# Squares of q and k laid out by head in a fused two-block transformer kernel, and the sums over them on VectorE

## The reference, cut to what matters

```python
def _l2norm(t):                     # HEADS = 16, EPS = 1e-12
    n = jnp.sqrt(jnp.sum(t * t, axis=-1, keepdims=True))
    return t / jnp.maximum(n, EPS)
q, k, v = (proj(Wq), proj(Wk), proj(Wv))   # (b, head, token, 8)
q = _l2norm(q)
k = _l2norm(k)
sim = jnp.einsum('bhid,bhjd->bhij', q, k) * SCALE
```

## Time and profile before

| | |
|---|---|
| median of 3 runs | 1092.72 us (1090.68 to 1095.87) |
| the profiled execution | 1093.79 us, of which the span from first to last instruction is 1092.0 us |
| granted TensorE clock, mean | 0.951 of full speed |
| busy: PE, DVE, ACT, POOL | 946.0, 877.3, 768.5, 281.8 us |
| sums of squares, line 1175 | 32 instructions, 32.4 us |
| squares, line 972 | 32 instructions, 19.3 us |

### The profile page before, as it was taken

One profiled execution on the slowest core, in us unless ns is written; L12 is line 12 of the kernel. 1 busy time (PEld: TensorE's weight loads), 2 busy tenths in 40 slices (PEclk: granted clock), 3 DMA queues, 4 the chain that ended last, 5 costly groups with the idle time before them and its releaser, 6 DMA issues.

```text
span 1092.0 us, 37313 instructions
## 1 busy us (share of the span) xinstructions
PE 946.0 (87%) x15889; PEld 516.0 (47%) x15889; DVE 877.3 (80%) x2112; ACT 768.5 (70%) x1042; POOL 281.8 (26%) x264
## 2 busy tenths in 40 slices
PE   4687978888989899999999999998989899899694
PEld 1333444444544445454555545454545455455352
DVE  3977767889788898989899898989898888864633
ACT  2165557677767778787777778887777778788581
POOL 6111213223133131322223132223223232222212
PEclk8598889899999999999999999999999999999797
DMA  5243413455417062442617162543628170405220
GB/s 148 76 97 99 119 45 85 118 127 129 128 57 189 22 190 57 138 119 84 172 48 198 36 186 54 144 106 104 152 69 186 41 195 22 119 3 127 72 57 20
DMA packets 94342, 112.95 MB, mean 103 GB/s; under 512 B 15200, under 2 KB 81888, under 8 KB 94176
## 3 DMA queue, kind: packets, MB, share of 16 engines
q1 hardware_dynamic: 94176, 110.56, 38.6%
HBM read 55.22 MB, written 54.53 MB: 100 GB/s over the span
## 4 chain that ended last, share of the span: by engine, by line
PE 44%; DVE 31%; ACT 15%; issue 6%; POOL 1%; DMA 1%; SPq 0%; DVEq 0%; POOLq 0%; ACTq 0%
PE acc L729 14%; DVE rowmax L1081 11%; ACT prob L930 10%; PE pool L712 6%; PE pool L595 4%; PE pool L643 4%; PE pool L762 3%; DVE xn L1039 3%; PE pool L784 3%; PE pool L609 3%; DVE stats L1027 2%; PE pool L770 2%; PE pool L659 2%; DVE rest_k L1052 2%; PE pool L681 2%
## 5 line engine op out<-in xcount | busy, mean ns | idle before, releaser
L930 ACT ACTIVATE prob<-pool 128x1024 f32<-128x1024 f32 x576 | 565.3, 1030 | 136.3 <-PE pool L659 132.8
L1081 DVE TENSOR_REDUCE rowmax<-pool 128x2 f32<-128x1024 f32 (+7 forms) x480 | 357.2, 791 | 64.9 <-PE pool L659 62.2
L729 PE MATMUL acc<-prob,vals_a 128*32 128x512 f32 (+7 forms) x2048 | 167.7, 422 | 0.2 <-ACT prob L930 0.2
L729 PE MATMUL acc<-prob,vals_b 128*32 128x512 f32 (+7 forms) x2048 | 162.8, 418 | 1.5 <-DVE turned_b L1117 1.1
L643 PE MATMUL pool<-stack_ka,stack_qa 48*64 48x512 bf16 (+7 forms) x2048 | 117.0, 301 | 39.7 <-ACT prob L930 12.7
L712 PE MATMUL pool<-stack_qa,stack_ka 51*64 51x512 bf16 (+7 forms) x2048 | 113.3, 301 | 32.6 <-DVE rowmax L1081 18.4
L659 PE MATMUL pool<-mask_t,ident_b 64*64 64x128 bf16 (+1 forms) x2304 | 129.5, 215 | 0.0
L712 PE MATMUL pool<-stack_qb,stack_kb 48*64 48x512 bf16 (+7 forms) x2048 | 112.4, 295 | 17.1 <-ACT prob L930 8.3
L643 PEld LDWEIGHTS pool<-stack_ka,stack_qa 48*64 48x64 bf16 x2048 | 42.8, 108 | 131.8 <-issue 46.8
L1292 POOL TENSOR_TENSOR rstd<-mv,minus_half 128x4 f32<-128x4 f32 x64 | 65.4, 1022 | 146.1 <-DVE mv L1034 146.1
L712 PEld LDWEIGHTS pool<-stack_qa,stack_ka 51*64 51x64 bf16 x2048 | 42.8, 108 | 88.2 <-issue 26.3
(11 more groups left out here) (129 smaller groups left out, 1380.5 us busy)
## 6 DMA issues: line engine op xcount, KB each, us to landing
stack_qa<-scratch_qa SPq DMA_DIRECT2D x64, 192.0 KB, 4.9
stack_ka<-scratch_ka SPq DMA_DIRECT2D x64, 192.0 KB, 4.9
stack_kb<-scratch_kb SPq DMA_DIRECT2D x64, 192.0 KB, 3.9
stack_qb<-scratch_qb SPq DMA_DIRECT2D x64, 192.0 KB, 4.8
scratch_qa<-parts_q SPq DMA_DIRECT2D x16, 384.0 KB, 2.8
scratch_ka<-parts_k SPq DMA_DIRECT2D x16, 384.0 KB, 4.8
scratch_qb<-parts_q SPq DMA_DIRECT2D x16, 384.0 KB, 2.6
scratch_kb<-parts_k SPq DMA_DIRECT2D x16, 384.0 KB, 2.9
```

Of the source, the lines that this page charges most:

```text
L729: last = eng.matmul(acc[32 * j:32 * j + 32, BLK * blk:T], vals[a][:, blk, GROUP * g + j, :], prob[n % NPROB][:, k, at:at + T - BLK * blk], ...
L930: eng.activation(prob[n % NPROB][:, :, :], place["unit", n][0][:, :, :], ACT.Exp, scale=scale).then_inc(S["exped"], 1)
L1081: last = eng.tensor_reduce(to, of, axis=AX.X, op=ALU.max)
```

## The change

The squares are written in the order (h d), a head's 8 components side by side, while they are read from PSUM in the order (d h) as they stand there. The sum reads them in the order in which they now lie. Nothing else is changed: the copy `raw`, the result `qk` of line 1207, all instruction counts, waits and the order of the steps are the same.

```diff
@@ class Scalar, project_qk @@
                     q.wait_ge(S["qk_made"], 2 * b + half + 1)
-                    eng.activation(qk[:, two, :, :].rearrange("p k a c -> p k (a c)"),
-                                   ps[:, :].rearrange("p (k c) -> p k c", k=2), ACT.Square)
+                    eng.activation(qk[:, two, :, :].rearrange("p k a (h d) -> p (k a) d h", d=D),
+                                   ps[:, :].rearrange("p (ka d h) -> p ka d h", d=D, h=HEADS), ACT.Square)
                     eng.activation(raw[:, two, :, :].rearrange("p k a c -> p k (a c)"),
                                    ps[:, :].rearrange("p (k c) -> p k c", k=2), ACT.Copy).then_inc(S["raw_qk"], 1)
@@ class Vector, project_qk @@
                     last = eng.tensor_reduce(
                         ssum[:, w * half:w * (half + 1)].rearrange("p (k h) -> p k h", k=4),
-                        qk[:, two, :, :].rearrange("p k a (d h) -> p (k a) h d", d=D), axis=AX.X, op=ALU.add)
+                        qk[:, two, :, :].rearrange("p k a (h d) -> p (k a) h d", d=D), axis=AX.X, op=ALU.add)
```

## The result

The changed kernel takes 1102.31 us (median of 4 runs, 1101.71 to 1103.76), against 1093.37 us before (median of 4 runs, 1090.68 to 1095.87): a ratio of 1.0086, with a 95% interval of 1.0061 to 1.0112. It is slower by about 9 us, where I had forecast 2.4 us less. The range ended at 1096 us, so the result lies outside it, at the rival that I had given 0.08.

A forecast was written before the change was run, and what follows sets the result against it. No engine is full; the chain runs 44% on PE, 31% on DVE, 15% on ACT. Seven shorter sums at four places save 2.45 us, 1093.79 to 1091.3 us (1090.3 for the median); range 1085.5 to 1096 us.

The forecast's parts named there:

- the rival that I had given 0.08: ScalarE's squares pay for scattered writes, 0.60 to 0.95 us each; 6.4 us slower, 1099.1 us; chance 0.08.
- the regular batches hide the sums: In seven batches of 60.7 us period, the 0.70 us saved before the row maxima becomes idle time; no gain.
- the rival by which every microsecond of VectorE counts: The schedule closes up behind the shorter sums in all 16 batches: 11.2 us less, 1081.5 us; chance 0.10.
- the idle time: VectorE's wait before the row maxima in regular batches, for line 659, would grow from 0.19 to 0.89 us.
- the four places: Batches at 146.47, 204.88, 296.91 and 1018.20 us where sums lie on the chain; seven instructions, 2.45 us saved.
- The new sum: VectorE's line 1175, reading neighbours, falls from 1035 ns to 0.68 us, 0.35 us less for each of 32.
- I take 0.60 us, no change.: ScalarE's squares, line 972, keep their 603 ns although their writes to SBUF are now spread.
- The two rows that I took as nearest: ScalarE's scattered writes at lines 916 (378 ns, 256 elements) and 845 (204 ns, 32 elements), showing no extra cost.
- The upper bound: Most that a ScalarE square could lengthen: VectorE's own excess, 0.35 us on 512 elements.
- the slower rival: Squares on ScalarE lengthen 0.35 us each; after a 0.30 us gap, 16 x 0.40 = 6.4 us slower; chance 0.08.
- the point from which it decides: About 0.15 us more per ScalarE square, where two fill the 0.30 us gap before the exponential.

The follow-up runs named there:

- the sums alone: Against the kernel before: squares written as before, only line 1175's sum reads neighbours (8 heads of one component); 1094.01 us, ratio 1.0008.
- the write alone: Against the kernel before: squares written by head as in the change, sum still reading at 64 bytes; 1103.27 us, ratio 1.0097.
- the run with one copy: Against the kernel before: short neighbour-reading sums, squares as before, plus one extra 512-element ScalarE copy behind the copies to raw; 1093.43 us, ratio 0.9997.
- the two kernels with short sums and fast squares: Neighbour-reading sums with squares as before (1094.01 us), and the changed kernel with ScalarE reading PSUM at steps and writing neighbours (1093.74 us).
- the kernel that joins the exchanged patterns and the semaphore: Against the changed kernel: ScalarE reads PSUM at steps, writes neighbours, and the square has its own semaphore; 1089.31 us, again 1089.32 us.
- the early semaphore: Against the kernel before: only a semaphore of the square's own, so sums start before the copy to raw ends; 1094.76 us, ratio 1.0016.

## Why the prediction was wrong

*What bounds the kernel; the regular batches hide the sums.* Right. With the sums alone the regular period stayed at 60.69 us, and the rival by which every microsecond of VectorE counts (ratio 0.990) is out. Only the idle time I had wrong, 0.56 us in place of 0.89, for the reason given below under the four places.

*The new sum.* Right in size and in reason: 0.684 us from the line through the row maxima, 0.686 us measured, with the 64 results still there. The excess was the distance of the reads.

*The squares: "I take 0.60 us, no change."* This step failed: the write's step was given no cost. Measured were 1116 ns, and the kernel with the write alone has the whole loss. The two rows that I took as nearest write in runs of 8 and of 2 values. In a run of 8 the elements share their lines; in runs of 2 at 16 bytes there are still two to a line, and the table above shows that two are nearly enough (0.65 us). Those rows could not speak of single elements. The upper bound failed as well: I took VectorE's 0.35 us, and ScalarE pays 0.51 us. The trace held the warning: VectorE's read at 64 bytes' step was a long row of the kernel before in which each element lay in a line of its own, and I had used it for the gain while I set it aside for the cost. The rule of the Trainium skill that I weighed against the rows was the better witness here.

*The price of the slower rival.* The mechanism was named. I had 0.35 us a square, a gap of 0.30 us on ScalarE and 16 x 0.40 = 6.4 us. Measured were 0.51 us a square, 0.94 us to the exponentials, a slack of 0.57 us, and 0.36 us in a regular batch. That 0.36 is near my 0.40, and the 6.65 us of the traces near my 6.4, is luck: a square priced too low and a slack taken too small cancelled. Outside the regular batches the loss comes through the sums as well as through the exponentials. I had also said that the shorter sum does not help; the write alone is 0.28 us a batch slower than the change. Of the point from which it decides I had said 0.15 us a square; the run with one copy shows that exponentials 0.52 us later in a batch, 0.26 us a square, still cost nothing in settled batches.

*The saving at the four places.* I counted 0.70 us for each pair. Only the last sum of a pair counts, since the second waits for ScalarE in any case: 4 x 0.35 = 1.4 us in place of 2.45. Between the first square and the end the two kernels with short sums and fast squares are 0.6 and 0.45 us shorter than the kernel before (946.0 and 946.2 against 946.65 us). Without the interval from the fourteenth batch to the fifteenth, which is 1.2 us longer in both at a lower clock (0.94 against 0.97), they are 1.8 and 1.7 us shorter, which fits 1.4 us. It does not show in the times, whose intervals of 0.9991 to 1.0025 and 0.9992 to 1.0022 hold nothing below -1 us.

*The chances.* The rival that came true had 0.08, and the range was drawn to leave it out. It had a row of single elements in lines of their own on its side and the forecast had none; something like 0.3 would have been the reading of these rows.

## What to carry to other kernels

A layout that helps the reader has to be paid by the writer: look which of the engines can make the jump on a side where it is free. Here the same tile costs ScalarE 0.60 us if it jumps in its PSUM reads and 1.11 us if it jumps in its SBUF writes.

For the price of an access pattern in SBUF a row counts as near only if it has as many elements to a line of 16 bytes, however alike the step looks; a row of another engine with the same sharing is nearer than one of the same engine with runs.

Time taken from an engine off the path is worth nothing, but time added to another engine is free only up to its slack. Ask for both, and for the second path behind the first.

## What the runs showed of the hardware

- ScalarE writing float32 to SBUF: 0.60 us for 512 elements at a step of 4 bytes, 0.65 at 8, 1.13 at 16, 1.12 at 32, 1.05 at 64. The copy that follows a slow write is longer too, 654 in place of 607 ns.
- VectorE reading float32 from SBUF: 0.69 us at 4 and 8 bytes, 1.10 and 1.11 at 16 and 32, 1.035 at 64.
- ScalarE reading PSUM at a step of 64 bytes costs nothing: 603 ns.
- Where TensorE's clock falls differs between two executions of the same kernel. In the two traces of the kernel that joins the exchanged patterns and the semaphore, the interval from the third batch's first square to the fourth's took 61.47 us at a mean granted clock of 1.00, and 62.52 us at 0.97. Between kernels too it moves single intervals by more than the change's part in them: the interval between the first squares of the fourteenth and fifteenth batch took 59.5 us before and 60.65 us with the sums alone. The busy times by stretch, first of the kernel before, where the last 3 us are at half the clock (columns: stretch, us, busy us and count of PE, PEld, DVE, ACT, POOL, then the granted clock, the share of DMA and GB/s):

```profile
936.00:940.00 4.00, 1.99 (x48) 1.23 (x52) 3.90 (x5) 2.18 (x4) 0.78 (x1) 0.96 0.21 72
940.00:943.00 3.00, 3.00 (x44) 0.98 (x35) 1.80 (x11) 1.94 (x2) 2.18 (x2) 0.50 0.46 153
```

then of the kernel with the sums alone, in the same place of the program:

```profile
933.00:937.00 4.00, 2.35 (x28) 0.94 (x32) 3.90 (x7) 1.53 (x3) 0.41 (x2) 0.62 0.28 92
937.00:941.00 4.00, 4.00 (x68) 1.67 (x59) 1.43 (x10) 2.21 (x3) 2.17 (x2) 0.53 0.51 169
```

In both TensorE had waited 2.2 us for the row maxima; in the one it started again at the full clock of 2.4 GHz and fell to 1.2 GHz about 1.7 us later, in the other it was at 1.2 GHz at once. With 1 us or more of this in a single interval, a difference of 0.1% can't be read from one trace.

What stays open: why the layout and the semaphore gain only together, and whether the early semaphore's 0.16% alone is more than a shift of such stretches. Nor is it shown how the loss outside the regular batches splits between late sums, late exponentials and the clock.
